# Key projections in waves of eight blocks with the norm chains behind them, and value weights in half slots

## The reference

```python
xn = _layernorm(x, axis=-1)
x = x + _L0_attn_ref(xn, Wq, Wk, Wv, Wo, ...) + _L0_ffn_ref(xn, ...)
# attention: 16 heads of 2 x 64
q = rope(x @ Wq.T); k = rope(x @ Wk.T); v = x @ Wv.T
p1 = softmax(q1 @ k1.T * scale); p2 = softmax(q2 @ k2.T * scale)
attn = rmsnorm(p1 @ v - lam * (p2 @ v)) * gamma * (1 - LAMBDA_INIT)
return attn.reshape(...) @ Wo.T
```

## Time and profile before

| what | value |
|---|---|
| median of two runs | 6253.58 us (6243.08 to 6264.09) |
| the profiled execution | 6235.3 us |
| span of its slowest core | 6233.7 us (all cores 6210.4 to 6233.7) |
| TensorE matmul busy | 4229.2 us, 68% of the span |
| ScalarE busy | 1734.5 us, 28% |
| VectorE busy | 1077.4 us, 17% |
| POOL busy | 207.7 us, 3% |
| mean granted TensorE clock | 0.823 |

### The profile page before, as it was taken

How to read it: one execution, slowest core, us unless ns; L and a number is a source line. 1 busy time by engine, 2 the same in 40 slices (tenths; PEclk the granted TensorE clock), 3 DMA queues, 4 the chain that set the end, 5 groups by cost and what they waited for, 6 DMA issues and landing times.

```text
span 6233.7 us, 47774 instructions; the slowest of 8 cores (6210.4 to 6233.7 us)
## 1 busy us (share of the span) xinstructions
PE 4229.2 (68%) x16260; PEld 1351.9 (22%) x16260; DVE 1077.4 (17%) x1876; ACT 1734.5 (28%) x1863; POOL 207.7 (3%) x402
## 2 busy tenths in 40 slices
PE   2557456545744575567787778888787887878877
PEld 0113112211211131122233333211111111111113
DVE  3330432143123302311101110000000000000002
ACT  1111111111120111100000000266666666666650
POOL 0000000000000000001101010000000000000000
PEclk7779677866876787689999999988888888888879
DMA  4245312421241122145576566400100001000006
GB/s 135 68 95 162 111 41 77 142 78 37 108 142 49 63 98 41 27 78 99 98 122 115 99 101 114 95 14 14 27 14 14 14 14 27 14 14 14 14 11 152
DMA packets 177300, 428.86 MB, mean 69 GB/s; under 512 B 75944, under 2 KB 75944, under 8 KB 170152
## 3 DMA queue, kind: packets, MB, share of 16 engines
q0 software_dynamic: 55872, 272.65, 20.9%
q1 hardware_dynamic: 121192, 153.16, 8.3%
HBM read 539.02 MB, written 58.72 MB: 96 GB/s over the span
## 4 chain that ended last, share of the span: by engine, by line
PE 62%; DVE 14%; ACT 10%; DMA 7%; issue 5%; DVEq 1%; ACTq 0%; SPq 0%; POOLq 0%; POOL 0%
PE ps_a L1051 9%; PE ps_a L1441 7%; PE ps_b L1278 6%; PE ps_a L1142 6%; PE ps_a L1147 5%; PE ps_a L1252 5%; PE ps_d L1288 5%; PE ps_b L1283 4%; PE ps_d L1292 4%; PE ps_a L289 2%; DMA xc<-xTb 2%; PE ps_b L1186 2%; PE ps_b L1193 2%; ACT e L1272 2%; DVE tswp_bf L233 2%
## 5 line engine op out<-in xcount | busy, mean ns | idle before, releaser
L1272 ACT ACTIVATE e<-ps_a,bias_sb 128x1024 bf16<-128x1024 f32 x1024 | 1141.1, 1114 | 456.5 <-PE ps_a L1257 450.9
L1142 PE MATMUL ps_a<-xn_bf,wffn 128*128 128x512 bf16 x1408 | 568.3, 404 | 277.8 <-DVE h_bf L1168 258.8
L252 PE MATMUL ps_d<-sq_b,mask_bf 128*1 128x512 bf16 x160 | 93.5, 584 | 707.6 <-ACT sq_b L247 523.9
L1147 PE MATMUL ps_a<-xn_bf,wffn 128*128 128x512 bf16 x1408 | 566.8, 403 | 0.0
L1252 PE MATMUL ps_a<-q_bf,ktb 64*128 64x512 bf16 x1024 | 415.0, 412 | 111.2 <-DVE xn_bf L1337 98.8
L1051 PE MATMUL ps_a<-xnb,wbuf 128*128 128x512 bf16 x1536 | 436.0, 455 | 77.3 <-DVE xnb L221 77.3
L1278 PE MATMUL ps_b<-e,vtb 128*128 128x512 bf16 x1024 | 403.2, 394 | 63.6 <-ACT e L1272 50.2
L231 ACT ACTIVATE qraw_bf<-ps_a 128x1024 bf16<-128x1024 f32 x80 | 81.9, 1024 | 1207.2 <-PE ps_a L1051 980.2
L1257 PE MATMUL ps_a<-q_bf,ktb 64*128 64x512 bf16 x1024 | 415.9, 413 | 0.0
L1283 PE MATMUL ps_b<-e,vtb 128*128 128x512 bf16 x1024 | 404.0, 394 | 0.0
L1292 PE MATMUL ps_d<-e,ones_col_bf 128*1 128x512 bf16 x1024 | 402.2, 393 | 0.0
(11 more groups left out here) (121 smaller groups left out, 3795.7 us busy)
## 6 DMA issues: line engine op xcount, KB each, us to landing
wffn<-gu POOLq DMA_DIRECT2D x176, 512.0 KB, 7.2
xc<-xTb SPq DMA_DIRECT2D x64, 1024.0 KB, 5.6
wvbuf<-wv_c POOLq DMA_DIRECT2D x28, 2048.0 KB, 10.7
wffn<-dn POOLq DMA_DIRECT2D x64, 704.0 KB, 9.8
wbuf<-wk_c POOLq DMA_DIRECT2D x48, 512.0 KB, 3.6
kT_s<-kstage SPq DMA_DIRECT2D x64, 256.0 KB, 2.4
v_s<-v_stage SPq DMA_DIRECT2D x32, 512.0 KB, 7.3
ktb<-kT_s SPq DMA_DIRECT2D x16, 1024.0 KB, 5.0
```

Of the source, the lines that this page charges most:

```text
L1142: p.emit("pe", lambda E, kch=kch, par=par, tile=tile, gsl=gsl: E.matmul(t["ps_a"][:, par * 1024: par * 1024 + 512], wffn[:, gsl * 2048 + k ...
L1147: mm = lambda E, kch=kch, par=par, tile=tile, usl=usl: E.matmul(t["ps_a"][:, par * 1024 + 512: par * 1024 + 1024], wffn[:, UOFF + usl * 20 ...
L1272: ev = p.inc("act", "ac", 1, lambda E, par=par, h=h: E.activation(t["e12"][:, par * 1024:(par + 1) * 1024], ps_a[:, par * 1024:(par + 1) * ...
```

## The change

In each chunk the 16 och are split into two waves of eight. In a wave TensorE does the matmuls of all eight och; after each, ScalarE copies the PSUM half into one of eight slots of a new tile `kraw` (128 x 8192, bf16). Only then does `consume_k` run for the eight och, one after the other, each from its slot, with the new `emit_rope_sb`, which has no PSUM copy. A copy of the second wave also waits until the rope of the first wave has read the slot. `wvbuf` shrinks from 16384 to 12288 columns: three slots of 4096, each half of what a slot held, and every group of value matmuls now takes two loads (and in the first half pass two cache writes) and waits for each half before its 32 matmuls.

```diff
+def emit_rope_sb(p, t, src_view, ctab, stab, ccol0, dst_bf, dst_col0):
+    sw, ta = t["tswp_bf"], t["tmpa_bf"]
+    p.inc("dve", "dv", 1, lambda E: E.stream_shuffle(sw[:], src_view, SWAP_MASK))
+    srcfree = p.inc("dve", "dv", 1, lambda E: E.tensor_tensor(
+        ta[:], src_view, ctab[:, ccol0:ccol0 + 1024], ALU.mult))
+    p.inc("dve", "dv", 1, lambda E: E.tensor_tensor(
+        sw[:], sw[:], stab[:, ccol0:ccol0 + 1024], ALU.mult))
+    wv = p.inc("dve", "dv", 1, lambda E: E.tensor_tensor(
+        dst_bf[:, dst_col0:dst_col0 + 1024], ta[:], sw[:], ALU.add))
+    return srcfree, wv
...
+    t["kraw"] = entk(nc.sbuf_tensor("kraw", [128, 8192], BF16, side="right"))
-    t["wvbuf"] = entk(nc.sbuf_tensor("wvbuf", [128, 16384], BF16, side="right"))
+    t["wvbuf"] = entk(nc.sbuf_tensor("wvbuf", [128, 12288], BF16, side="right"))
-    vwring = Ring(p, "rvw", 2, "pool")
+    vwring = Ring(p, "rvw", 3, "pool")
...
-        for och in range(16):
-            par = och % 2
...
-            kwring.consumed(i, "pe")
-            p.wait("dve", "pe", mmv)
-            free[par] = consume_k(och, mmv)
+        kraw_free = {}
+        for wave in range(2):
+            cpvs = []
+            for o8 in range(8):
+                och = wave * 8 + o8
+                par = och % 2
...
+                kwring.consumed(i, "pe")
+                p.wait("act", "pe", mmv)
+                if wave == 1:
+                    p.wait("act", "dv", kraw_free[o8])
+                cpv = p.inc("act", "ac", 1, lambda E, par=par, o8=o8: E.activation(
+                    t["kraw"][:, o8 * 1024:(o8 + 1) * 1024],
+                    t["ps_a"][:, par * 1024:(par + 1) * 1024], AF.Copy))
+                cpvs.append(cpv)
+                free[par] = {"ac": cpv}
+            for o8 in range(8):
+                och = wave * 8 + o8
+                p.wait("dve", "ac", cpvs[o8])
+                kraw_free[o8] = consume_k(och, o8)
...
-            if fill_cache and halfq == 0:
-                i, slot, key = ring.load(... wvbuf[:, s * 8192:(s + 1) * 8192], in_=wv_hbm[dvq])
+            slots = []
+            for wh in range(2):
+                if fill_cache and halfq == 0:
+                    i, slot, key = ring.load(... wvbuf[:, s * 4096:(s + 1) * 4096],
+                        in_=wv_hbm[dvq][:, wh * 4096:(wh + 1) * 4096])
+                    p.wait("pool", *key)
+                    wcv = p.inc("pool", f"rvw{slot}", 16, ... out=wv_cache[dvq][:, wh * 4096:...])
...
+            for wh in range(2):
+                i, slot, key = slots[wh]
+                p.wait("pe", key[0], key[1])
+                for kch in range(wh * 8, wh * 8 + 8):
...
+                ring.consumed(i, "pe")
```

More of the change, by code:

```diff
@@ L1013, in build_F, with consume_k @@
         psfree = emit_ln(p, t, xTb[:, c0:c0 + 1024], xn_dst, 1024, 0, ring=lnring)
-        def consume_k(och, mmv, chunk=chunk, c0=c0):
+        def consume_k(och, o8, chunk=chunk, c0=c0):
             gidx = chunk * 16 + och
@@ L1020, in consume_k @@
                 p.wait("dve", "ac", ksq_done[gidx - 2])
-            psfree_kv, wv_ = emit_rope(p, t, t["ps_a"][:, half * 1024:(half + 1) * 1024],
-                                       t["ctab"], t["stab"], c0, t["kstage"], half * 1024)
+            srcfree, wv_ = emit_rope_sb(p, t, t["kraw"][:, o8 * 1024:(o8 + 1) * 1024],
+                                        t["ctab"], t["stab"], c0, t["kstage"], half * 1024)
             emit_headnorm(p, t, t["kstage"], half * 1024, och, statbase=0)
@@ L1029, in consume_k @@
                 in_=t["kstage"][:, half * 1024:(half + 1) * 1024])))
-            return {psfree_kv[0]: psfree_kv[1]}
+            return srcfree
         free = [dict(psfree), dict(psfree)]
-        for och in range(16):
-            par = och % 2
[L1035 to L1059, removed]
-            kwring.consumed(i, "pe")
-            p.wait("dve", "pe", mmv)
-            free[par] = consume_k(och, mmv)
@@ new lines, in build_F @@
+        kraw_free = {}
[4 more added lines that the diff above has]
+                par = och % 2
+                if chunk == 0:
+                    i, slot, key = kwring.load(lambda s: (lambda E, och=och, s=s: E.dma_start(
+                        out=t["wbuf"][:, s * 2048:(s + 1) * 2048], in_=wk[och])))
+                    p.wait("pool", *key)
+                    wcv = p.inc("pool", f"rkw{slot}", 16, lambda E, och=och, s=slot: E.dma_start(
+                        out=wk_c[och], in_=t["wbuf"][:, s * 2048:(s + 1) * 2048]))
+                    kwring.done[i][f"rkw{slot}"] = wcv
+                else:
+                    i, slot, key = kwring.load(lambda s: (lambda E, och=och, s=s: E.dma_start(
+                        out=t["wbuf"][:, s * 2048:(s + 1) * 2048], in_=wk_c[och])))
+                for sem, val in free[par].items():
+                    p.wait("pe", sem, val)
+                p.wait("pe", key[0], key[1])
+                for kch in range(KCH):
+                    for half in range(2):
+                        mm = lambda E, och=och, kch=kch, half=half, par=par, slot=slot, xn_dst=xn_dst: E.matmul(
+                            t["ps_a"][:, par * 1024 + half * 512: par * 1024 + (half + 1) * 512],
+                            t["wbuf"][:, slot * 2048 + kch * 128: slot * 2048 + (kch + 1) * 128],
+                            xn_dst[:, kch * 1024 + half * 512: kch * 1024 + (half + 1) * 512],
+                            start=(kch == 0), stop=(kch == KCH - 1))
+                        if kch == KCH - 1 and half == 1:
+                            mmv = p.inc("pe", "pe", 1, mm)
+                        else:
+                            p.emit("pe", mm)
+                kwring.consumed(i, "pe")
[11 more added lines that the diff above has]
+                kraw_free[o8] = consume_k(och, o8)
@@ new lines, in emit_vproj_cache @@
+            for wh in range(2):
+                if fill_cache and halfq == 0:
+                    i, slot, key = ring.load(lambda s: (lambda E, dvq=dvq, wh=wh, s=s: E.dma_start(
+                        out=t["wvbuf"][:, s * 4096:(s + 1) * 4096],
+                        in_=wv_hbm[dvq][:, wh * 4096:(wh + 1) * 4096])))
+                    p.wait("pool", *key)
+                    wcv = p.inc("pool", f"rvw{slot}", 16, lambda E, dvq=dvq, wh=wh, s=slot: E.dma_start(
+                        out=wv_cache[dvq][:, wh * 4096:(wh + 1) * 4096],
+                        in_=t["wvbuf"][:, s * 4096:(s + 1) * 4096]))
+                    ring.done[i][f"rvw{slot}"] = wcv
+                else:
+                    i, slot, key = ring.load(lambda s: (lambda E, dvq=dvq, wh=wh, s=s: E.dma_start(
+                        out=t["wvbuf"][:, s * 4096:(s + 1) * 4096],
+                        in_=wv_cache[dvq][:, wh * 4096:(wh + 1) * 4096])))
+                slots.append((i, slot, key))
@@ L1435, in emit_vproj_cache @@
             for sem, val in free.items():
                 p.wait("pe", sem, val)
[L1437 to L1449, removed]
@@ L1450, in emit_vproj_cache @@
-            ring.consumed(i, "pe")
+            for wh in range(2):
+                i, slot, key = slots[wh]
+                p.wait("pe", key[0], key[1])
+                for kch in range(wh * 8, wh * 8 + 8):
+                    for tc in range(4):
+                        tok = xn_col0 + halfq * 512 + tc * 128
+                        mm = lambda E, kch=kch, tc=tc, tok=tok, slot=slot: E.matmul(
+                            vps(tc),
+                            xn_bf[:, kch * xn_seg + tok: kch * xn_seg + tok + 128],
+                            t["wvbuf"][:, slot * 4096 + (kch % 8) * 512:
+                                       slot * 4096 + (kch % 8 + 1) * 512],
+                            start=(kch == 0), stop=(kch == KCH - 1))
+                        if kch == wh * 8 + 7 and tc == 3:
+                            p.inc("pe", "pe", 1, mm)
+                        else:
+                            p.emit("pe", mm)
+                ring.consumed(i, "pe")
```

## The result

The changed kernel's median is 6203.75 us (6137.04 to 6461.82 over 11 runs), that of the kernel before 6258.08 us (6228.97 to 6471.22 over 10). The ratio is 0.9841, 95% interval 0.9797 to 0.9884, 99 us off 6258 (73 to 127). The change is clearly faster; whether by more or by less than 2%, the interval leaves open. In the profiled execution of the changed kernel (6190.39 us) I read die 1, and in it core 4, the core shown of before.

What follows compares the result with a forecast made beforehand. Each key block was read as a closed 10.73 us chain plus a 9.10 us group slowed by TensorE's lower clock level. Savings of 100 - 4 - 7 = 89 us gave 6146 to 6164.6, set at 6155 us, range 6120 to 6205.

Steps and rivals of the forecast that it cites:

- Eight groups in a row: Key projection: a wave's matmuls take 57.4 us, only the first group starting at the lower clock level.
- The tail: Key projection: eight serial norm chains after a wave's last group, 11.67 us a step, 88.5 us in all.
- the bound that I had named: Key waves: 103 us saved if the first mask pair after a wave still runs at the upper clock level.
- The reordering itself loses: Key tails: copies leave the path, seven of eight second reductions come onto it, costing 2.7 us per wave.
- Keys together: Key projections: 100 us saved over eight waves, less 4 us for late key weights in chunk 0.
- Key weights in chunk 0: Chunk 0 key waves: cast loads overlapping cache writes make groups late, 4 us lost (0 to 12).
- Value weights in chunk 0: Chunk 0 value stage: half loads beside cache writes land late, 7 us lost (gain of 2 to loss of 10).
- The sum: Whole kernel: 100 - 4 - 7 = 89 us saved, forecast 6155 us, chance 0.82.
- (a): Key tails: mask pairs keep the clock at 2.4 GHz, 71 us more saved, 6084 us; chance 0.05.
- (b): Value stage, chunks 1 to 3: half-slot ring runs dry, 42 us lost, 6210 us, no change; chance 0.06.
- (c): Key waves: dense matmuls held at a lower level, 8.4 us a group, 6239 us, no change; chance 0.04.
- (d): Key waves: key weight loads are the bound, 379 us lost at 14.2 us each, 6534 us; chance 0.03.

Runs made afterwards that it cites:

- filler runs: Kernel before, order unchanged, plus unread matmuls: 24 after each key group, ratio 0.9805; then 26, and 9 more between the mask pairs, ratio 0.9694.
- halves-alone run: Kernel before with only the value weights in three half slots, key projection untouched: 6231.56 us at best, against 6232.33 for the fastest of before.
- first filler run: Kernel before, order unchanged, with 24 unread matmuls after each key group: ratio 0.9805, interval 0.9522 to 1.0088.

## Why the prediction was right, step by step

- **Eight groups in a row.** 57.4 us predicted, 57.8 measured. The first group starts at the lower level, the rest runs at 0.216 us a matmul, with no wait in chunks 1 to 3 (56.9 to 57.9 us over their six waves).
- **The tail.** 88.5 predicted, 89.1 and 89.6 measured. A step is 11.76 instead of 11.67, since 0.17 us and not 0.10 pass between the last small tensor_tensor and the next shuffle. The first mask pair ran at the upper level (0.77 us until VectorE starts instead of 1.18), the bound that I had named; from the second on all of them in chunk 1 are at the lower.
- **The reordering itself loses.** 2.7 us a wave predicted. A tail of 89.4 in the mean against eight chains of 10.73 is 3.6. The filler runs showed from the other side that the gain is the clock's.
- **Keys together.** 100 less 4 predicted, 88 measured on core 4 and 90 in the median of die 1. On core 4 the tails take 7 us more than forecast and the eight waves of matmuls with chunk 0's waits nearly 3; about 2 come back because the windows of the earlier trace rows were 2.3 us short.
- **Key weights in chunk 0.** 4 us predicted (0 to 12), about 7 measured: the two waves of chunk 0 take 62.3 and 60.1 us. On core 4 the waits on wk sum to 5.6 us, the longest 1.76. The cast load that lay alone in 5.61 us takes up to 7.98 (166.00 to 173.98) in a wave, more than the 7.2 that I had taken as the most, as POOL's timeline of the same core shows:

```profile
152.19 0.53 POOL L1053 DMA_DIRECT2D wbuf<-wk  x1 [113.84 <-PE ps_a L1067]
157.87 0.54 POOL L1056 DMA_DIRECT2D wk_c<-wbuf  x1 [5.16 <-DMA wbuf<-wk]
159.09 0.53 POOL L1053 DMA_DIRECT2D wbuf<-wk  x1 [0.69 <-PE ps_a L1067]
165.11 0.54 POOL L1056 DMA_DIRECT2D wk_c<-wbuf  x1 [5.48 <-DMA wbuf<-wk]
166.00 0.53 POOL L1053 DMA_DIRECT2D wbuf<-wk  x1 [0.36 <-issue]
173.98 0.54 POOL L1056 DMA_DIRECT2D wk_c<-wbuf  x1 [7.45 <-DMA wbuf<-wk]
```

- **Value weights in chunk 0: the term that was mis-sized.** 7 us lost predicted, 0.6 gained measured on core 4 (138.92 against 139.56). I had priced a half beside a write at 12.0 to 13.4 us by a line through two sizes plus half the extra of a whole one:

```profile
453.11 0.53 POOL L1453 DMA_DIRECT2D wvbuf<-wv  x1 [72.58 <-PE ps_a L1474]
461.18 0.54 POOL L1457 DMA_DIRECT2D wv_c<-wvbuf  x1 [7.54 <-DMA wvbuf<-wv]
461.79 0.53 POOL L1453 DMA_DIRECT2D wvbuf<-wv  x1
472.07 0.54 POOL L1457 DMA_DIRECT2D wv_c<-wvbuf  x1 [9.75 <-DMA wvbuf<-wv]
```

  A half takes 8.1 us alone and 10.3 beside a write (9.9 to 11.8 over the four), so the stage waits for one load by 1.62 us where it waited 1.98. The other cores of die 1 lie between 137.1 and 143.2 us (137.1 and 140.5 before), so die 1 as a whole loses about 1 us. The halves-alone run, where the stage cost up to 7 us more, shows that the price depends on the core and on what runs ahead; what sets it there was not tried.
- **The sum.** 89 us predicted, 99 by the ratio (73 to 127), 102 on the medians of die 1. The forecast of 6155 us is 0.9835 of the median of before; the ratio is 0.9841. That the figures come so close is in part luck: the keys gave 6 to 8 us less than their terms, and the value weights cost 6 to 8 less than theirs. The mechanism, the clock level gained in the groups and a little lost in the tails, is as forecast.
- **Rivals.** (a) the level up through the tail: no, mask matmuls at 0.58 us from the second pair on. (b) the value ring dry: no waits on wv_c in chunks 1 to 3 of core 4. (c) no change by a lower level for dense waves: no on core 4, where eight groups take 57.8 us and groups of 8.4 would take 67. (d) the key ring: a median landing of 3.6 us and 8.0 at most, no wait in chunks 1 to 3 of core 4.
- **A reading that was wrong.** The prediction has a granted clock of 0.9 and more wherever keys or queries aren't projected. The row of PEclk in the earlier trace rows reads 8 over most of its second half. No term of the sum used it.
- **What I weighed too little.** I had the ledger of a tail (11.67 a step, 2.7 us lost a wave) in hand and did not draw from it that a shorter wave would be better, or that an order with one block of lag would hide the whole chain.

## What to carry to other kernels

When matmul groups are longer than columns times the rate of the upper clock level, look for the pause ahead of them, and price the pause twice: once for its length and once for the group that starts cold. Before you batch work to make an engine dense, write down which hand-overs leave the path and which come onto it per batch; here batches of eight bought 99 us, of two 165, and running the chain of one block under the matmuls of the next bought 526 to 660 on the keys and some 830 with the queries. A wait inside a chain on a scratch buffer (here the second mask pair on the first pair's reductions) is worth a second buffer as soon as the chain is off the path.

## What the runs showed of the hardware that was not expected

The level falls in shorter pauses than I took it to, but no length of pause decides it. In the first filler run, core 2, a mask matmul runs at 0.58 or 0.59 us after 2.29 us of pause in 42 blocks and at 0.38 in 20. In the order with one block of lag, core 5, the same pause between the pairs leaves the upper level in 59 of 63. The value stage keeps its level over most pauses of 3.07 us: in chunk 1 of core 4 of the changed kernel all groups after the first take 13.97. And it can fall with hardly a pause before it, as in a layer norm of the same core:

```profile
1713.47 0.38 PE L188 MATMUL ps_d<-xbb,ones_col_bf 128*1 128x512 bf16 x1 [2.54 <-ACT x2b L184]
1713.68 0.38 PE L191 MATMUL ps_d<-x2b,ones_col_bf 128*1 128x512 bf16 x1
1714.19 0.58 PE L188 MATMUL ps_d<-xbb,ones_col_bf 128*1 128x512 bf16 x1
```

Between the last two there are 0.13 us. The level outlived the pause of 2.54 us and fell behind one of 0.13. So what TensorE did before the last pause must count as well. How, the runs don't settle.
